# Feed-forward phases: the residual added by an identity product on TensorE, and a factor folded into the product with the inverse

## The reference

```python
def fp4_quant_dequant(x):            # blocks of 16 along the last dim
    scale = max(max(abs(block)) / 6.0, 1e-12)
    xn = xb / scale
    idx = jnp.searchsorted(_MID, jnp.abs(xn))
    q = _GRID[idx] * jnp.sign(xn) * scale

gate = fp4_linear(x, w_gate)         # both operands quantised, 128 -> 352
y = fp4_linear(x, w_up)
h = jax.nn.silu(gate) * y
return fp4_linear(h, w_down)         # 352 -> 128

x = x + 0.5 * _L0_ffn_ref(_layernorm(x), w_gate, w_up, w_down)
```

## Time and profile before

| | us |
|---|---|
| Median of 3 runs | 1586.96 |
| Lowest, highest | 1584.87, 1587.45 |
| The profiled execution | 1589.33 |
| Its span, first to last instruction | 1587.6 |
| TensorE busy in it | 1202.7 |
| VectorE busy | 997.5 |
| ScalarE busy | 782.1 |
| GpSimd busy | 592.3 |

### The profile page before, as it was taken

One profiled execution on the slowest core, in us unless ns is written; L12 is line 12 of the kernel. 1 busy time (PEld: TensorE's weight loads), 2 busy tenths in 40 slices (PEclk: granted clock), 3 DMA queues, 4 the chain that ended last, 5 costly groups with the idle time before them and its releaser, 6 DMA issues.

```text
span 1587.6 us, 34432 instructions
## 1 busy us (share of the span) xinstructions
PE 1202.7 (76%) x11393; PEld 912.2 (57%) x11394; DVE 997.5 (63%) x1974; ACT 782.1 (49%) x1333; POOL 592.3 (37%) x859
## 2 busy tenths in 40 slices
PE   0677469999956777289999915999997637999992
PEld 0355346666634556278888812455554526888882
DVE  5799589998847995922332357899896373233333
ACT  0444225555554442255555551666666424555556
POOL 2122131221102220056666614676775104666561
PEclk9998669999989896589999956999999757999996
DMA  8000034232300001011111133334232101111115
GB/s 256 8 0 0 1 61 63 44 60 52 51 2 1 0 0 54 1 36 41 42 41 41 40 112 68 69 56 78 57 73 36 54 0 29 42 41 41 40 42 172
DMA packets 161959, 75.58 MB, mean 48 GB/s; under 512 B 126539, under 2 KB 153940, under 8 KB 161876
## 3 DMA queue, kind: packets, MB, share of 16 engines
q1 hardware_dynamic: 152404, 55.06, 15.9%
q0 software_dynamic: 9472, 19.42, 4.1%
HBM read 28.69 MB, written 15.86 MB: 28 GB/s over the span
## 4 chain that ended last, share of the span: by engine, by line
PE 44%; DVE 29%; issue 10%; ACT 8%; POOL 3%; DMA 3%; SPq 1%; DVEq 1%; POOLq 0%; ACTq 0%
PE PS L990 19%; DVE pt L1114 5%; PE PS L656 4%; PE PS L358 2%; ACT xTs L1045 2%; DVE sg L790 2%; PE PS L638 2%; DVE m L790 2%; PE PS L622 2%; PE PS L575 2%; PE PS L950 2%; PE PS L610 1%; ACT pt L1070 1%; SPq L882 1%; DVE q_amax L266 1%
## 5 line engine op out<-in xcount | busy, mean ns | idle before, releaser
L990 PE MATMUL PS<-xTs,pt 128*128 128x128 f32 x2336 | 302.6, 284 | 22.3 <-ACT xTs L1045 7.4
L990 PEld LDWEIGHTS PS<-xTs,pt 128*128 128x128 f32 x2336 | 275.5, 194 | 49.4 <-ACT xTs L1045 49.4
L1114 DVE TENSOR_TENSOR pt<-pt,PS 128x512 f32<-128x512 f32 x146 | 100.4, 688 | 295.4 <-PE PS L990 295.4
L715 ACT ACTIVATE pt<-PS 128x768 f32<-128x768 f32 (+1 forms) x256 | 227.6, 917 | 111.4 <-PE PS L638 59.5
L1227 POOL DMA_INDIRECT xs<-rows,src x152 | 147.3, 969 | 192.4 <-DVE src L1108 146.7
L1236 POOL DMA_INDIRECT outs<-ys,dst x144 | 142.0, 986 | 146.0 <-DVE ys L1122 140.0
L1050 ACT ACTIVATE pt<-PS 128x512 f32<-128x512 f32 x146 | 87.2, 597 | 181.9 <-PE PS L990 181.6
L1039 ACT ACTIVATE pt<-wgu 128x1024 f32 x148 | 156.3, 1057 | 27.3 <-issue 6.9
L790 DVE TENSOR_REDUCE m<-PS 128x4 f32<-128x1024 f32 x128 | 149.2, 1218 | 13.5 <-PE PS L575 12.9
L1010 PE MATMUL PS<-wdn,pt 128*128 x1152 | 152.2, 275 | 0.0
L1010 PEld LDWEIGHTS PS<-wdn,pt 128*128 128x128 f32 x1152 | 140.0, 192 | 0.0
(11 more groups left out here) (228 smaller groups left out, 2117.1 us busy)
## 6 DMA issues: line engine op xcount, KB each, us to landing
pt<-outs SPq DMA_DIRECT2D x16, 512.0 KB, 5.0
rows<-qT SPq DMA_DIRECT2D x12, 256.0 KB, 2.4
xs<-rows,src POOLq DMA_INDIRECT x152
outs<-ys,dst POOLq DMA_INDIRECT x144, 2.3
wgu<-in_L_ffn_w_gate SPq DMA_DIRECT2D x1, 2048.0 KB
wgu<-in_L_ffn_w_up SPq DMA_DIRECT2D x1, 2048.0 KB
wdn<-in_L_ffn_w_down SPq DMA_DIRECT2D x8, 256.0 KB
qT<-hqT SPq DMA_DIRECT2D x128, 4.0 KB
```

Source lines behind the costliest of these rows:

```text
L715: s.activation(k.pt[:, a % 4, :, 0:w], k.PS[:, self.bank:self.bank + 2, 0:w], ACT.Exp, scale=self.scale).then_inc(self.s_p, 1)
L990: last = t.matmul(k.PS[:, 1 + 2 * p + w, c * P:(c + 1) * P], k.wst[:, 1 - p, w, c * P:(c + 1) * P], k.xTs[:, p, :], start=True, stop=True)
L1114: v.tensor_tensor(k.hs[:, p, :], k.sgs[:, p, :], k.PS[:, 2 + 2 * p, :], ALU.mult).then_inc(self.s_h, 1)
```

## The change

In the feed-forward phases, x is added to the down product by TensorE: after the three chunks of each tile, one more product, of the identity with the tile of X, is accumulated in bank 7. ScalarE copies the bank back to X (after L403, before the normalisation) and signals `s_added`; VectorE only waits for that and takes the statistics. The factor 0.5 goes into the copy of `wdT`. The multiplication L273 is dropped, and L274 becomes a `scalar_tensor_tensor` with the constant as its scalar.

```diff
             ch.run(v.reciprocal(inv, scale))
-            ch.run(v.tensor_scalar(inv, inv, -NUDGE, None, ALU.mult))
-            last = v.tensor_tensor(xn.rearrange("p (n k) -> p n k", k=BLK), blocks,
-                                   inv.unsqueeze(2).broadcast_to([P, n, BLK]), ALU.mult)
-            last.then_inc(self.s_xn_read, 1)
+            v.scalar_tensor_tensor(xn.rearrange("p (n k) -> p n k", k=BLK), blocks, -NUDGE,
+                                   inv.unsqueeze(2).broadcast_to([P, n, BLK]), ALU.mult,
+                                   ALU.mult).then_inc(self.s_xn_read, 1)
 
             if self.has(z - 4):
-                self.add(eng, z - 4)
+                eng.wait_ge(self.s_added, x0 + z - 3)
+                for j in range(2):
+                    bn_stats(k, 2 * (z - 4) + j)
 
-        self.walk(eng, fn, ch, 5)
-
-    def add(self, eng, i):
-        k, v = self.k, self.k.nc.vector
-        eng.wait_ge(self.s_y_ps, self.x0 + i + 1)
-        v.scalar_tensor_tensor(k.X[:, ds(2 * i, 2), :], k.PS[:, 7, 0:256].rearrange("p (a b) -> p a b", a=2),
-                               0.5, k.X[:, ds(2 * i, 2), :], ALU.mult, ALU.add).then_inc(self.s_added, 1)
-        eng.wait_ge(self.s_added, self.x0 + i + 1)
-        for j in range(2):
-            bn_stats(k, 2 * i + j)
+        self.walk(eng, fn, ch, 4)
 
                 for j in range(2):
                     for c, (o, w) in enumerate(HC):
-                        last = t.matmul(k.PS[:, 7, j * D:(j + 1) * D], k.hqT[0:w, j, c, :], k.wdT[0:w, c, :],
-                                        start=c == 0, stop=c == 2)
+                        t.matmul(k.PS[:, 7, j * D:(j + 1) * D], k.hqT[0:w, j, c, :], k.wdT[0:w, c, :],
+                                 start=c == 0, stop=False)
+                    last = t.matmul(k.PS[:, 7, j * D:(j + 1) * D], k.ident[:, :], k.X[:, ds(2 * (z - 3) + j, 1), :].squeeze(1),
+                                    start=False, stop=True)
                 last.then_inc(self.s_y_ps, 1)
 
                 s.activation(k.xqT[:, :], k.PS[:, 4, 0:256], ACT.Copy).then_inc(self.s_xqT, 1)
+            if self.has(z - 3):
+                eng.wait_ge(self.s_y_ps, x0 + z - 2)
+                s.activation(k.X[:, ds(2 * (z - 3), 2), :], k.PS[:, 7, 0:256].rearrange("p (a b) -> p a b", a=2),
+                             ACT.Copy).then_inc(self.s_added, 1)
+            if self.has(z):
                 if not isinstance(z, int) or z + 2 < self.N:
 
-                last = nc.vector.tensor_copy(k.wdT[0:m, c, :], k.PS[0:m, 2, c * P:(c + 1) * P])
+                last = nc.vector.tensor_scalar(k.wdT[0:m, c, :], k.PS[0:m, 2, c * P:(c + 1) * P], 0.5, None, ALU.mult)
```

## The result

The changed kernel took 1577.99 us in the median (1576.42 to 1579.49, five runs) beside 1587.05 us for the kernel before (1584.87 to 1590.09, five runs): a ratio of 0.9941, 95% interval 0.9927 to 0.9956, that is 7.0 to 11.6 us less. The predicted 1583.0 us was 5 us too high, and the range ended at 1578.5, just above what came. The profiled execution of after took 1577.99 us, its span is 1576.3 us; that of before had a span of 1587.6 us.

The account below looks back on a forecast made before the run. VectorE's chain was taken to bound the feed-forward phases. The sum -7.7 (L273) + 2.0 (bursts) + 0.3 (single down groups) + 1.4 (tails) = -4.0 us, off the median 1586.96, gave 1583.0 us; range 1578.5 to 1589.0 us.

Parts of the forecast that it names:

- the fold: Feed-forward steps on VectorE: dropping L273 into a product of three takes 34 x 0.225 = 7.7 us off.
- the bursts: Gate/up groups wholly at TensorE's low clock: two of four stay, 2.0 us back, plus 0.3 us for single down groups.
- the tails: End of each feed-forward phase, without cover: identity products add 0.48 us at high and 0.88 us at low clock, 1.4 us together.
- The price of L273: VectorE's chain: the small multiplication costs the distance between its start and L274's, 0.225 us, in 17 of 18 steps per phase.
- The fused product: L274 on VectorE as a product of three: same duration, cost 0; the rival that it is slower had chance 0.05.
- The add's removal: L299 leaving VectorE, 0.42 us for each of 32 pairs: worth nothing, as the square on ScalarE covers it.
- The copy on ScalarE: New PSUM read behind L403: 0.38 us, next operation 0.28 us behind it, cost 0 in the ordinary step.
- the two identity products: Four more TensorE instructions per down group: 0.48 us at high or 0.88 us at low clock, cost 0 in ordinary steps.
- no bursts: Rival: no gate/up groups at the low clock in the changed kernel's feed-forward steps, 1580.3 us; chance 0.24.
- ScalarE in the way: Rival: the new copy delays the square in ordinary steps, up to 0.28 us each, 1590.2 us at worst; chance 0.08.
- TensorE as the bound: Rival: steps after a low-clock group stay bound by TensorE, 2.6 us each, 1596 us with five; chance 0.06.
- What the low clock cost the old kernel: Old kernel's feed-forward bursts: 0.1 to 0.2 us each, 0.4 us in the sum for the case without bursts.

Follow-up runs that it names:

- e2: Only the moved add (identity products, copy on ScalarE) against the kernel before, L273 kept: 1587.71 us, ratio 1.0005.
- e10: The whole change run again, on one chip with the folded factor alone, against the kernel before: 1578.48 us, ratio 0.9937.
- e9: The folded factor alone run again, on one chip with the whole change, against the kernel before: 1578.53 us, ratio 0.9944.
- e8: The kernel before with a second small multiplication of the inverse, by 1.0, behind L273: 1597.34 us, ratio 1.0065; a second profiled run took 1594.24 us.
- e14: The whole change plus 32 unused products in the set-up, which move TensorE's later instruction loads: 1575.91 us, ratio 0.9937 to the kernel before.
- e4: The folded factor plus unused identity products behind each step's down products, add still on VectorE, against the kernel before: 1580.05 us, ratio 0.9951.
- e6: The whole change plus the next step's block maximum of x taken under the square: 1573.4 us, ratio 0.9910 to the kernel before.
- e15: The whole change with x's block maximum taken a step ahead, plus 32 unused set-up products: 1572.80 us, ratio 0.9917 to the kernel before.
- e1: Only the folded factor against the kernel before, L273 gone and the add still on VectorE: 1576.91 us, ratio 0.9931.
- e13: The folded factor alone plus 32 unused products in the set-up: 1578.54 us, ratio 0.9952 to the kernel before.
- e3: The kernel before plus two unused identity products behind each step's down products: 1585.72 us, ratio 0.9991.

## Why the prediction was wrong, point by point

Its main term, the fold, holds on the chain: 7.7 us, where the fold alone gave 7.2 to 10.4 us in the medians. What failed are the two terms that it added for the low clock, +2.3 us for the bursts and +1.4 us for the tails: 3.7 us, the larger part of them for the work that the moved add puts on TensorE and ScalarE. In their place e2 has a ratio of 1.0005 (1.3 us less to 2.7 us more) for the moved add alone, and on one chip the whole change and the fold alone differ by 0.05 us in the median (e10 and e9).

- **The price of L273, 0.225 us on the chain: right.** Reciprocal to fused product stays 0.56 us, the product 1.16 us, and in e8 the starts of the small operations and the product are 0.22 and 0.23 us apart. The Trainium skill (VectorE: DVE Perf Modes, The TRN2 errata) led to an estimate of 92 ns for the operation; the trace of e8 has 0.19 us, as that of before had. The same section says that its row gives too little and that the fixed term was measured at about 150 cycles, by which the estimate would have been 188 ns: that agrees with the trace.
- **The fused product costs nothing more: right.** The median duration by source is 1157 ns, against 1158 ns.
- **The add's removal is worth nothing at the square: right but for a trifle.** The gap from product to rounding is 2.22 to 2.23 us in both. In every second loop step before had 2.32 us, the square starting 1.28 instead of 1.19 us behind the product; a register operation stands on ScalarE's sequencer there. In the view of line L394 of before it is (count, duration min/median/max in ns, first and last start):

```profile
L394 ACTq ALU_OP  x10: 35/35/35, 78.0 to 571.6; - x10
```

  With the X addresses moved it is gone from the line of the square: 0.085 us in ten steps, 0.85 us. The prediction had put the moved address computations at 0, at most some tenths.
- **The copy on ScalarE, the two identity products: right.** 0.38 us with no wait in the ordinary step; the down group 2.06 us, against the 2.09 foreseen.
- **The bursts at the low clock: the first step that failed.** The prediction kept two of four and charged 2.3 us for them. None stayed in any of the three profiles of the whole change (after, e10, e14). The argument "a busier engine should fall less often" pointed the right way, and its size was a guess; no row of before could size it. The rival "no bursts" (chance 0.24) is the case that happened, and its 1580.3 us was still 2.3 us too high, for the two reasons that follow. The Trainium skill (TensorE: Matmul & The Clock Gate, Part 1) says that activity releases the throttle; by that rule, the counts of e2 to e4 agree.
- **The tails: the second step that failed, with the wrong sign.** +1.4 us were charged, on the assumption that the last groups keep their clock. They didn't: 13.32 and 12.00 us became 11.51 and 11.52, 2.3 us less. In the first phase the last down group alone had cost 2.93 - 1.60 = 1.33 us at the low clock, the transposes 1.54 - 0.88 = 0.66 us, in both phases; with 0.48 for the identities, and 0.22 for the L273 that also stands in each tail, the sum for both is about 2.1 us less. That the added work did this isn't shown: e4, e6 and e15 have it too, and their first tails are at the low clock again (13.7 us each).
- **ScalarE in the way, TensorE as the bound: neither came.** In the ordinary step the square starts 1.19 us behind the product (75.32 to 76.51), and no step of after stays with TensorE.
- **What the low clock cost the old kernel: too small.** The prediction allowed it 0.4 us, four bursts of 0.1 to 0.2. By the distances between the block maxima of before and after, less the price of L273 and the register operation, four steps with a late Silu cost 0.18, 0.20, 0.27 and 0.29 us, and step 16 of the first phase 0.54 us (6.91 us, where the second phase and both further profiles of before have 6.37): 1.5 us without the tails.

The loops then add up: 10.2 us shorter, of which 32 x 0.225 = 7.2, the 0.85 of the square, the 1.5 us just named, and 0.29 and 0.28 us in the second step of each phase, where the gate/up group took 4.77 and 4.34 us in place of 5.06 and 4.62. That last item is scatter of the clock at a phase's start: the second step of the first phase ranges from 8.26 to 8.81 us in the three profiles of the whole change. With the tails it is the 12.5 us seen. In the medians 9.1 us remain; the attention over windows takes some of it back, 1.2 us in the profiled pair and up to 4 against other profiles of before. The forecast was 8.5 us off in the two phases, some 7.5 us of it by the low clock, and 5 us off in the median. That it came out closer in the median is luck: the untouched phases took part of the gain back.

The fold alone brings as much as the whole in the medians. In the profiles the moved add wins 2 to 6 us in its own phases, and the attention over windows, which it doesn't touch, is 2 to 4 us longer (after against e1, e10 against e9, e14 against e13). The prediction named this only as something that could make it wrong ("shifts of a microsecond or more in the attention and expert phases").

**Open.** The fold alone gave 10.4, 9.6 and (padded) 7.2 us in three batches, where its own term is 7.7; its profiles have 2 to 4 groups at the low clock and tails between 11.8 and 13.1 us, and their phases are 5.2 to 10.5 us shorter than in one or the other profile of before. A second small multiplication cost 9.7 us in the median and 6 in the phases of its profile. Which of the transfers that a load crosses land late (142 of 266) isn't known, nor what gives the phase its length beside them: e13, e3 and before speak against the one place alone. And that the added products keep the clock up rests on counts in single profiles: 3 to 5 groups at the low clock in three of before, 8 in two of e8, 2 to 4 with the fold alone, 0 or 1 in all eight with added products in the steps. For the tails it doesn't hold.

## What to carry to other kernels

A small operation on the engine that sets the pace is priced by the distance between starts, times the steps; removing one was the whole gain here, while an operation that already lies under another engine's work gives only idle time. Work of the chain moved into the other engine's time pays: with the block maximum of the next step there the median is 14.3 us below before, where the whole change without it had 9 to 10. But with the add still in its place it is 13.3 us below before on the same chip, so try it without making room first. When an engine goes at the low clock in some steps, give that time its own terms in the loop and in the tail, and carry both cases through the sum, the tail too, in place of one guess for each. And look at the phases that the change doesn't touch: their length differed by 3 to 5 us between single profiles of programs with the same code there, as much as half the gain.

## What the runs showed of the hardware beyond that

- The granted clock of TensorE stayed high with slightly more work: 0.48 us per step of 7.6 us more, and the gate/up groups that went wholly at the low clock (5.06 us in place of 2.63) went from 4 to 0. A step longer by 0.22 us with the same work (e8) had 8. That was worth little by itself: e3 with 1 such group had a ratio of 0.9991. In a loop such a group cost the step of VectorE from nothing (most of e8's) to 0.54 us (step 16 of before's first phase).
- Transposing transfers that no load of instructions crossed landed within 3.6 us (822 of 822, in 17 profiles); of the 266 that one crossed, 142 took longer, up to 5.4 us. The packets of these loads have 16,384 or 8,192 bytes. At the one place shown a transfer took 4.9 in place of 3.1 us, and VectorE waited 1.87 in place of 0.84 us.
- A register operation of 35 ns on ScalarE's sequencer ahead of an activation that is wanted at once came with a start 0.09 us later; none of the page's busy times shows it.
